# Running the first layernorm statistics one tile ahead of the second in a transformer block's preparation stage

## The chip, the cores and the metric

The kernel runs on all 8 NeuronCores of one Trainium2 chip. Each core computes one element of the batch on its own, with no exchange between cores. The metric is the device time in microseconds (us) of the slowest core. A core has these engines, each with its own in-order instruction queue: TensorE (PE in the profile, its weight loads PEld), VectorE (DVE), ScalarE (ACT), GpSimd (POOL) and SyncE (SP, which here issues DMA transfers). ScalarE issues DMAs too (ACTq). Engines wait for each other by semaphores.

## The reference, cut to what matters

x is 8 x 4096 x 2048 in float32; a core has one 4096 x 2048 part of it.

```python
xn = _layernorm(x, axis=-1)                    # (x - mean) / sqrt(var + 1e-5)
x = x + attn(xn, Wq, bq, Bq, Aq, ..., Ao) + ffn(xn, gamma, beta, weight, bias, alpha)

# attn: q, k, v, out projections with rank-16 LoRA updates, 16 heads of 128, softmax
# ffn:
mu = jnp.mean(x, axis=-1, keepdims=True)       # x is xn here: a second layernorm
var = jnp.mean(jnp.square(x - mu), axis=-1, keepdims=True)
xn = (x - mu) * jax.lax.rsqrt(var + LN_EPS) * gamma + beta
a = jnp.sign(xn)
signed_w = jnp.sign(weight - jnp.mean(weight, axis=1, keepdims=True))
out = (jnp.einsum('bsi,oi->bso', a, signed_w) + bias) * alpha
```

So each row of x is normalized once for the attention (LN1), and the result is normalized again (LN2), scaled, shifted and reduced to its sign for the ffn.

## The kernel before, in words

The program is a list of stages (`_phase0` to `_phase5`), each written out as straight code for all engines. Between two stages `_join` lets every engine wait for all semaphores, so no stage overlaps the next. `_phase0` loads constants and transposes the small LoRA matrices. `_phase1`, which the change touches, makes both normalized inputs. `_phase2` computes the q, k and v projections, `_phase3` the attention, `_phase4` the output projection and `_phase5` the ffn product.

`_phase1` first broadcasts gamma and beta to all partitions (`gb_g`, `gb_b`). Then it walks over NT = 32 tiles of 128 rows x 2048 columns. For tile t:

- SP loads the float32 rows of the next tile into `xf[(t+1)%2]` (L296), once the last readers of that buffer are through.
- `stats_pass` on `xf` (LN1): VectorE sums the row (L242), makes the mean (L244) and its negative (L246). ScalarE squares the centred row with an accumulated sum (L252, `Square`; the squared row itself goes into a scratch tile that nobody reads, here `abf`). VectorE divides by D (L258); ScalarE takes Ln (L260) and Exp with -0.5 (L263), which give 1/sqrt(var + eps). VectorE makes the offset (L266).
- VectorE writes the normalized row `xn32` (L304).
- `stats_pass` on `xn32` (LN2): the same lines again, with `xnbf` as scratch. Between its Square and its Ln, ScalarE copies `xn32` to bfloat16 `xnbf` (L312, handed in as `mid=_cast`).
- VectorE normalizes `xn32` in place (L319), multiplies by gamma (L323) and adds beta (L325). ScalarE writes its sign to `abf` (L327).
- TensorE transposes `xnbf` in 16 blocks through the PSUM tiles `ptrA` and `ptrB` (L333, L345), ScalarE copies them out into `xn_fm` (L338, L350). The same happens with `abf` (L359, L373) into `a_acc` (L366, L378). Every second tile, ScalarE issues the store of `a_acc` to `s_a` (L389).

All the small per-row statistics lie in the eight columns of one tile, `stat`. The order of work on each engine is the order in which the code stands: nothing reorders it.

Of the kernel before, what the change touches and what calls it, by code (L numbers as in the profile page):

```python
# [34 lines left out]
def build_nc(T, D):  # L35
# [3 lines left out]
    NT = T // 128  # L39
# [3 lines left out]
    INV_D = 1.0 / D  # L43
# [5 lines left out]
    nc = bass.Bass("TRN2", target_bir_lowering=False)  # L49
# [176 lines left out]
    def _phase1(sync):  # L226
        ldx = [S("p1_ldx0"), S("p1_ldx1")]
        dv = S("p1_dv")
        ac = S("p1_ac")
        pe = S("p1_pe")  # L230
        sta = S("p1_sta")
        evA = S("p1_evA")
        evB = S("p1_evB")
        xf_last = {}
        abf_free = [0]
        xnbf_free = [0]

        def stats_pass(src, scratch, act_dv_wait=None, act_pe_wait=None,
                       dv_wait=None, mid=None):
            if dv_wait is not None:  # L240
                nc.vector.wait_ge(dv.h, dv_wait)
            v_sum = dv.inc(nc.vector.reduce_sum(stat[:, 0:1], src, axis=AX.X))  # L242
            nc.vector.wait_ge(dv.h, v_sum)
            v_mu = dv.inc(nc.vector.tensor_scalar_mul(stat[:, 2:3], stat[:, 0:1], INV_D))  # L244
            nc.vector.wait_ge(dv.h, v_mu)
            v_nm = dv.inc(nc.vector.tensor_scalar_mul(stat[:, 3:4], stat[:, 2:3], -1.0))  # L246
# [5 lines left out]
            a_sq = ac.inc(nc.scalar.activation(scratch, src, AF.Square,  # L252
                                               bias=stat[:, 3:4],
                                               accum_out=stat[:, 1:2]))
            if mid is not None:
                mid()
            nc.vector.wait_ge(ac.h, a_sq)
            v_var = dv.inc(nc.vector.tensor_scalar_mul(stat[:, 4:5], stat[:, 1:2], INV_D))  # L258
            nc.scalar.wait_ge(dv.h, v_var)
            a_ln = ac.inc(nc.scalar.activation(stat[:, 7:8], stat[:, 4:5], AF.Ln,  # L260
                                               bias=EPS))
            nc.scalar.wait_ge(ac.h, a_ln)
            a_r = ac.inc(nc.scalar.activation(stat[:, 5:6], stat[:, 7:8], AF.Exp,  # L263
                                              scale=-0.5))
# [21 lines left out]
        sync.wait_ge(pe.h, pe.v)  # L286
        ldx[0].dinc(sync.dma_start(xf[0].ap(), x_d.ap()[0:128, :]))

        for t in range(NT):
# [9 lines left out]
            nc.vector.wait_ge(ldx[sl].h, ldx[sl].v)  # L299
            nc.scalar.wait_ge(ldx[sl].h, ldx[sl].v)  # L300
# [6 lines left out]
            xf_last[t] = (v_xn, a_sq1)  # L307
# [6 lines left out]
            v_nmr2, a_sq2 = stats_pass(xn32.ap(), xnbf.ap(), act_dv_wait=v_xn,  # L314
                                       act_pe_wait=xnbf_free[0], dv_wait=v_xn,
                                       mid=_cast)
            nc.vector.wait_ge(dv.h, v_xn)
# [881 lines left out]
```

## Time and profile before

| what | value |
|---|---|
| median of 3 runs | 8460.73 us (8460.21 to 8728.11) |
| time of the profiled execution | 8459.73 us |
| its span, first to last instruction of the slowest core | 8457.9 us |
| spans of the 8 cores | 8446.6 to 8457.9 us |
| mean granted TensorE clock, every core | 0.838 |
| busy share of the span: PE, PEld, DVE, ACT | 66%, 26%, 37%, 32% |
| stages by start, from the timeline | `_phase1` loop 136 us, `_phase2` 953 us, `_phase3` about 2850 us, `_phase4` and `_phase5` from about 7000 us |

The profile is of one execution, on its slowest core; its span is 1.8 us shorter than the time measured for that execution. "Busy" is the time in which an engine executes; what it waited for stands in brackets behind an instruction of the timeline. The granted clock is 1.00 for TensorE's full 2.4 GHz and 0.50 for 1.2 GHz, averaged over a stretch.

### The profile page before, as it was taken

The numbers are of one execution on the slowest core, as the hardware profiler recorded it, in microseconds if no ns is written. First come the engines' busy times: TensorE is split into PE (matmuls) and PEld (weight loads), VectorE is DVE, ScalarE is ACT, GpSimd is POOL, SyncE is SP. The second block draws the span as 40 slices with busy tenths as digits, with TensorE's granted clock in tenths as the row PEclk, the third lists the DMA queues.
The fourth block names the chain that finished last, engine by engine and source line by source line (L and its number), as shares of the span: only waits on it lengthen the run. The fifth ranks groups of instructions, "written<-read, shape, count | busy, mean of one in ns | idle before, by whom it ended". The sixth has DMA issues, their size and how long they took to land.

```text
span 8457.9 us, 66068 instructions; the slowest of 8 cores (8446.6 to 8457.9 us)
## 1 busy us (share of the span) xinstructions
PE 5556.4 (66%) x22685; PEld 2235.6 (26%) x23096; DVE 3161.8 (37%) x2750; ACT 2664.3 (32%) x2610; POOL 3.7 (0%) x17
## 2 busy tenths in 40 slices
PE   1111488888888766666666666666666665996499
PEld 0111233333333222222222222222222222332243
DVE  3555311211111244444444444444444444113433
ACT  1444200000000255455555555555555552000000
POOL 0000000000000000000000000000000000000000
PEclk9999989889898877777777777777777776997699
DMA  1111111111111100000000000000000003442344
GB/s 35 60 64 60 52 58 52 57 53 52 56 54 56 46 19 5 19 20 19 19 15 9 19 19 20 19 5 19 19 20 19 5 4 115 149 149 103 126 167 149
DMA packets 171860, 424.87 MB, mean 50 GB/s; under 512 B 26005, under 2 KB 107925, under 8 KB 142869
## 3 DMA queue, kind: packets, MB, share of 16 engines
q1 hardware_dynamic: 80922, 269.60, 9.7%
q10 hardware_dynamic: 90624, 151.02, 4.8%
q8 instruction: 204, 3.34, 0.2%
q14 instruction: 110, 0.90, 0.0%
HBM read 269.58 MB, written 150.99 MB: 50 GB/s over the span
## 4 chain that ended last, share of the span: by engine, by line
PE 55%; DVE 23%; issue 11%; ACT 8%; DMA 1%; ACTq 1%; DVEq 1%; SPq 0%
PE sg L743 11%; PE avp L778 9%; PE pgB L502 8%; PE pgA L502 8%; DVE ptree L810 7%; PE pa L945 5%; PE pf L1111 5%; ACT pT L766 4%; DVE ptree L802 3%; DVE rec L622 3%; PE ptrW L480 1%; DVE obuf L613 1%; PE avp L616 1%; DVE stat L242 1%; DVE xn L323 1%
## 5 line engine op out<-in xcount | busy, mean ns | idle before, releaser
L766 ACT ACTIVATE pT<-sg,negc 128x1024 bf16<-128x1024 f32 x2048 | 2100.3, 1132 | 1699.3 <-DVE ostg L601 1504.7
L743 PE MATMUL sg<-qT,kT 128*128 128x512 bf16 x3997 | 1335.3, 427 | 492.4 <-ACT pT L766 480.6
L778 PE MATMUL avp<-pT,vh 128*128 128x512 bf16 x4019 | 1313.5, 413 | 112.1 <-ACT pT L766 105.6
L789 DVE TENSOR_TENSOR ptree<-pT 128x4096 bf16<-128x4096 bf16 x128 | 293.4, 2292 | 1762.3 <-ACT pT L766 1762.3
L743 PEld LDWEIGHTS sg<-qT,kT 128*128 128x128 bf16 x4096 | 389.4, 105 | 1318.3 <-issue 1076.8
L502 PE MATMUL pgB<-xn_fm,wT 128*128 128x512 bf16 x3000 | 706.7, 398 | 42.1 <-DVE wT L487 34.5
L502 PE MATMUL pgA<-xn_fm,wT 128*128 128x512 bf16 x3000 | 706.4, 398 | 41.8 <-DVE wT L487 34.1
L664 ACT ACTIVATE sq<-kT 128x4096 bf16<-128x4096 bf16 x16 | 58.9, 3683 | 1876.8 <-DMA qT<-s_qT 1876.8
L810 DVE TENSOR_TENSOR ptree<-ptree 128x4096 bf16<-128x4096 bf16 (+3 forms) x512 | 593.1, 1158 | 64.4 <-DVE ptree L802 23.1
L778 PEld LDWEIGHTS avp<-pT,vh 128*128 128x128 bf16 x4096 | 409.0, 106 | 777.1 <-issue 469.2
L616 PE MATMUL avp<-ptree,ones_bfc 128*1 128x512 bf16 x128 | 74.9, 585 | 723.4 <-DVE obuf L613 723.4
L622 DVE RECIPROCAL rec<-avp 1x512 f32<-1x512 f32 x128 | 428.2, 3346 | 107.6 <-PE avp L616 107.6
L945 PE MATMUL pa<-woT,o_sp 128*128 128x512 bf16 x2000 | 458.9, 380 | 11.3 <-ACT oBs L927 8.3
L1111 PE MATMUL pf<-swT,a_sp 128*128 128x512 bf16 x2005 | 456.3, 381 | 8.1 <-issue 6.6
L502 PEld LDWEIGHTS pgB<-xn_fm,wT 128*128 128x128 bf16 x3072 | 306.8, 102 | 436.4 <-issue 120.7
L502 PEld LDWEIGHTS pgA<-xn_fm,wT 128*128 128x128 bf16 x3072 | 306.8, 102 | 435.9 <-issue 119.8
L802 DVE TENSOR_TENSOR ptree<-pT 128x4096 bf16<-128x4096 bf16 x128 | 293.4, 2292 | 220.9 <-ACT pT L766 220.9
L333 PE MATMUL ptrA<-ident,xnbf 128*128 128x128 bf16 x256 | 32.4, 307 | 443.5 <-ACT stat L260 415.9
L594 PE MATMUL avp<-rec,ones_f32r 1*128 1x512 f32 x256 | 265.1, 1136 | 1.6 <-DVE rec L622 1.6
L945 PEld LDWEIGHTS pa<-woT,o_sp 128*128 128x128 bf16 x2048 | 189.9, 98 | 273.1 <-issue 61.5
L963 DVE TENSOR_TENSOR res<-pa,x_sp 128x1024 f32<-128x1024 f32 x64 | 78.4, 1224 | 486.7 <-PE pa L955 472.1
L1111 PEld LDWEIGHTS pf<-swT,a_sp 128*128 128x128 bf16 x2048 | 190.2, 98 | 243.2 <-issue 32.8
(120 smaller groups left out, 3276.5 us busy)
## 6 DMA issues: line engine op xcount, KB each, us to landing
xf<-x SPq DMA_DIRECT2D x32, 1024.0 KB, 4.9
x_sp<-x SPq DMA_DIRECT2D x32, 1024.0 KB, 6.5
out<-res ACTq DMA_DIRECT2D x64, 512.0 KB, 4.6
ord<-out SPq DMA_DIRECT2D x32, 1024.0 KB, 6.6
out<-res4b ACTq DMA_DIRECT2D x64, 512.0 KB, 4.4
s_a<-a_acc ACTq DMA_DIRECT2D x16, 1024.0 KB, 5.7
wbuf<-wq SPq DMA_DIRECT2D x16, 1024.0 KB, 5.9
wbuf<-wk SPq DMA_DIRECT2D x16, 1024.0 KB, 6.0
```

What stands on the lines that cost most here:

```text
L502: pe.inc(nc.tensor.matmul(pg[:, k * 512:(k + 1) * 512], wT[sl][:, ic * 128:(ic + 1) * 128], xn_fm[:, ic * T + tc * 512: ic * T + (tc + 1) ...
L594: pv = pe.inc(nc.tensor.matmul(avp[cur_qsl][:], ones_f32r.ap(), rec2[pqsl][0:1, :], start=True, stop=True))
L616: ptree_mm[pqsl] = pe.inc(nc.tensor.matmul(avp[pqsl][0:1, 0:512], ones_bfc.ap(), ptree2[pqsl][:, 0:512], start=True, stop=True, skip_group ...
L622: v_rec = dv.inc(nc.vector.reciprocal(rec2[pqsl][0:1, :], avp[pqsl][0:1, 0:512]))
L743: ins = nc.tensor.matmul(sg3[b][:, j * 512:(j + 1) * 512], kT_b[sl][:, kt * 128:(kt + 1) * 128], qT_b[sl][:, qq0:qq0 + 512], start=True, s ...
L766: e = ac.inc(nc.scalar.activation(pT2[qsl][:, g * 1024:(g + 1) * 1024], sg3[s_bank[g]][:], AF.Exp, bias=negc2[sl].ap()))
L778: pe.inc(nc.tensor.matmul(avp[qsl][:], vh2[sl][:, kt * 128:(kt + 1) * 128], pT2[qsl][:, kt * 512:(kt + 1) * 512], start=(kt == 0), stop=(k ...
L789: tree_a[0] = dv.inc(nc.vector.tensor_tensor(ptree2[qsl][:, 0:wq // 2], pT2[qsl][:, 0:wq // 2], pT2[qsl][:, wq:wq + wq // 2], ALU.add))
L802: v_part = dv.inc(nc.vector.tensor_tensor(ptree2[qsl][:, w // 2:w], pT2[qsl][:, w // 2:w], pT2[qsl][:, w + w // 2:2 * w], ALU.add))
L810: v_part = dv.inc(nc.vector.tensor_tensor(ptree2[qsl][:, 0:w // 2], ptree2[qsl][:, 0:w // 2], ptree2[qsl][:, w // 2:w], ALU.add))
L945: pe.inc(nc.tensor.matmul(pa[psl][:, ocs * 512:(ocs + 1) * 512], o_sp[sl][:, ic * 512 + tt * 128: ic * 512 + tt * 128 + 128], woT[:, ic * ...
L1111: pe.inc(nc.tensor.matmul(pf[psl][:, ocs * 512:(ocs + 1) * 512], a_sp[sl][:, ic * 512 + tt * 128: ic * 512 + tt * 128 + 128], swT[:, ic * ...
```

## The change

`stats_pass` is cut in two: `stats_head` (sum, mean, negative mean, Square and, where given, the copy) and `stats_tail` (variance, Ln, Exp, offset). LN2 gets a statistics tile of its own, `stat2`. The head of LN1 for tile t+1 is put behind the head of LN2 for tile t. The tail of LN1 for tile t+1 stands behind the Sign of tile t. The normalization of tile t+1 (`vxn[t+1]`) is the last thing in the body of tile t, behind the transposes and the evictions. LN1's Square now writes its unused squares in float32 into the other `xf` buffer (`xf[1 - s]`) instead of in bfloat16 into `abf`. The load of x for tile t+1 waits for LN1's Square of tile t, since that writes into the buffer that is loaded. Line numbers below are of the changed file.

```diff
+    stat2 = es_p1.enter_context(nc.sbuf_tensor("stat2", [128, 8], F32))
...
+        def stats_head(src_ap, scratch, sb, act_dv_wait=None, act_pe_wait=None,
+                       dv_wait=None, mid=None, nm_ac_wait=None):
...
+            if nm_ac_wait:
+                nc.vector.wait_ge(ac.h, nm_ac_wait)
+            v_nm = dv.inc(nc.vector.tensor_scalar_mul(sb[:, 3:4], sb[:, 2:3], -1.0))
...
+        def ln1_head(t, pe_wait=None):
+            s = t % 2
+            nc.vector.wait_ge(ldx[s].h, ldx[s].v)
+            nc.scalar.wait_ge(ldx[s].h, ldx[s].v)
+            return stats_head(
+                xf[s].ap(), xf[1 - s].ap(), stat,
+                act_dv_wait=(vxn[t - 1] if t >= 1 else None),
+                act_pe_wait=pe_wait,
+                nm_ac_wait=(sq1[t - 1] if t >= 1 else 0))
...
             if t + 1 < NT:
                 if t >= 1:
-                    pdv, pac = xf_last[t - 1]
-                    sync.wait_ge(dv.h, pdv)
-                    sync.wait_ge(ac.h, pac)
+                    sync.wait_ge(dv.h, vxn[t - 1])
+                sync.wait_ge(ac.h, sq1[t])
                 ldx[(t + 1) % 2].dinc(sync.dma_start(
...
-            v_nmr, a_sq1 = stats_pass(xf[sl].ap(), abf.ap(),
-                                      act_pe_wait=abf_free[0])
-            nc.vector.wait_ge(dv.h, v_nmr)
-            v_xn = dv.inc(nc.vector.tensor_scalar(
-                xn32.ap(), xf[sl].ap(), stat[:, 5:6], stat[:, 6:7],
-                ALU.mult, ALU.add))
...
+            a_sq2 = stats_head(xn32.ap(), xnbf.ap(), stat2,
+                               act_dv_wait=vxn[t], act_pe_wait=xnbf_free[0],
+                               dv_wait=vxn[t], mid=_cast,
+                               nm_ac_wait=sq2_prev[0])
+            sq2_prev[0] = a_sq2
+            if t + 1 < NT:
+                sq1[t + 1] = ln1_head(t + 1)
+            v_nmr2 = stats_tail(stat2, a_sq2)
...
             nc.scalar.wait_ge(dv.h, v_b)
+            nc.scalar.wait_ge(pe.h, abf_free[0])
             a_s = ac.inc(nc.scalar.activation(abf.ap(), xn32.ap(), AF.Sign))
+            if t + 1 < NT:
+                nmr1[t + 1] = stats_tail(stat, sq1[t + 1])
...
+            if t + 1 < NT:
+                nc.vector.wait_ge(dv.h, nmr1[t + 1])
+                nc.vector.wait_ge(ac.h, a_s)
+                vxn[t + 1] = dv.inc(nc.vector.tensor_scalar(
+                    xn32.ap(), xf[(t + 1) % 2].ap(), stat[:, 5:6], stat[:, 6:7],
+                    ALU.mult, ALU.add))
```

VectorE's queue before, from the LN1 normalization of tile 1 to the sum of the next tile's x; `xf0` and `xf1` are the two load buffers, `p1_dv`, `p1_ac`, `p1_pe` count what VectorE, ScalarE and TensorE have done:

```order
L304 TENSOR_SCALAR xn32<-xf1,stat 128x2048 [waits p1_dv]
L242 TENSOR_REDUCE stat<-xn32 128x1 [waits p1_dv]
L244 TENSOR_SCALAR stat<-stat 128x1 [waits p1_dv]
L246 TENSOR_SCALAR stat<-stat 128x1 [waits p1_dv]
L258 TENSOR_SCALAR stat<-stat 128x1 [waits p1_ac]
L266 TENSOR_SCALAR stat<-stat 128x1 [waits p1_ac]
L319 TENSOR_SCALAR xn32<-xn32,stat 128x2048 [waits p1_dv]
L323 TENSOR_TENSOR xn32<-xn32,gb_g 128x2048 [waits p1_dv]
L325 TENSOR_TENSOR xn32<-xn32,gb_b 128x2048 [waits p1_dv]
L242 TENSOR_REDUCE stat<-xf0 128x1 [waits p1_ldx0]
```

The same stretch of VectorE's queue in the changed kernel:

```order
L422 TENSOR_SCALAR xn32<-xf1,stat 128x2048 [waits p1_dv,p1_ac]
L246 TENSOR_REDUCE stat2<-xn32 128x1 [waits p1_dv]
L248 TENSOR_SCALAR stat2<-stat2 128x1 [waits p1_dv]
L252 TENSOR_SCALAR stat2<-stat2 128x1 [waits p1_dv,p1_ac]
L246 TENSOR_REDUCE stat<-xf0 128x1 [waits p1_ldx0]
L248 TENSOR_SCALAR stat<-stat 128x1 [waits p1_dv]
L252 TENSOR_SCALAR stat<-stat 128x1 [waits p1_dv,p1_ac]
L267 TENSOR_SCALAR stat2<-stat2 128x1 [waits p1_ac]
L275 TENSOR_SCALAR stat2<-stat2 128x1 [waits p1_ac]
L341 TENSOR_SCALAR xn32<-xn32,stat2 128x2048 [waits p1_dv]
L345 TENSOR_TENSOR xn32<-xn32,gb_g 128x2048 [waits p1_dv]
L347 TENSOR_TENSOR xn32<-xn32,gb_b 128x2048 [waits p1_dv]
```

The sum over the next tile's x moved from behind the beta addition to the place between LN2's negative mean and LN2's variance; the variance and offset of that next tile follow behind the beta addition.

ScalarE's queue before, from the bfloat16 copy of tile 1 to the Ln of tile 2:

```order
L312 ACTIVATE xnbf<-xn32 128x2048 [waits p1_ac]
L260 ACTIVATE stat<-stat 128x1 [waits p1_dv]
L263 ACTIVATE stat<-stat 128x1 [waits p1_ac]
L327 ACTIVATE abf<-xn32 128x2048 [waits p1_dv]
L338 ACTIVATE xn_fm<-ptrA 128x8x128 [waits p1_pe]
L350 ACTIVATE xn_fm<-ptrB 128x8x128 [waits p1_pe]
L366 ACTIVATE a_acc<-ptrA 128x8x128 [waits p1_pe]
L378 ACTIVATE a_acc<-ptrB 128x8x128 [waits p1_pe]
L389 DMA s_a<-a_acc 128x16x256 [waits p1_evA,p1_evB]
L252 ACTIVATE abf,stat<-xf0,stat 128x2048 [waits p1_ldx0,p1_pe,p1_dv]
L260 ACTIVATE stat<-stat 128x1 [waits p1_dv]
```

The same stretch of ScalarE's queue in the changed kernel:

```order
L328 ACTIVATE xnbf<-xn32 128x2048 [waits p1_ac]
L258 ACTIVATE xf1,stat<-xf0,stat 128x2048 [waits p1_ldx0,p1_dv]
L269 ACTIVATE stat2<-stat2 128x1 [waits p1_dv]
L272 ACTIVATE stat2<-stat2 128x1 [waits p1_ac]
L350 ACTIVATE abf<-xn32 128x2048 [waits p1_dv,p1_pe]
L269 ACTIVATE stat<-stat 128x1 [waits p1_dv]
L272 ACTIVATE stat<-stat 128x1 [waits p1_ac]
L363 ACTIVATE xn_fm<-ptrA 128x8x128 [waits p1_pe]
L375 ACTIVATE xn_fm<-ptrB 128x8x128 [waits p1_pe]
L391 ACTIVATE a_acc<-ptrA 128x8x128 [waits p1_pe]
L403 ACTIVATE a_acc<-ptrB 128x8x128 [waits p1_pe]
L414 DMA s_a<-a_acc 128x16x256 [waits p1_evA,p1_evB]
```

The next tile's Square moved from behind the evictions and the store to the place between the copy and LN2's Ln; the next tile's Ln and Exp stand between the Sign and the evictions. TensorE's queue is the same in both kernels, and SP's has the same transfers with the one changed wait.

## Rows read from the trace of the kernel before

**Rows 1.** Windows of core 0: busy us (and count) PE, PEld, DVE, ACT, POOL; PEclk, DMA, GB/s

```profile
136.00:952.00 816.00, 121.33 (x1024) 101.77 (x1024) 419.43 (x448) 397.21 (x448) 0.00 (x0) 1.00 0.19 60
952.00:1400.00 448.00, 383.14 (x1716) 171.21 (x1749) 78.77 (x64) 4.74 (x8) 0.00 (x0) 0.91 0.17 55
...
2400.00:2850.00 450.00, 388.72 (x1741) 171.45 (x1775) 85.41 (x68) 0.00 (x0) 0.00 (x0) 0.90 0.15 49
...
2950.00:3600.00 650.00, 411.90 (x1417) 144.34 (x1444) 299.43 (x224) 345.29 (x332) 0.00 (x0) 0.76 0.04 14
```

**Rows 2.** The tile `xf`: durations in ns min/median/max, first and last start in us

```profile
L304 DVE TENSOR_SCALAR xn<-xf,stat x32: 1345/1346/1347, 142.2 to 925.8; 128x2048 f32<-128x2048 f32 x32
...
DMA to landing us min/median/max: 4.7/4.9/9.2
```

**Rows 3.** Timeline of one tile that issues no store: start us, us, instruction

```profile
304.87 2.29 DVE L323 TENSOR_TENSOR xn<-xn,gb_g 128x2048 f32<-128x2048 f32 x1
307.27 2.29 DVE L325 TENSOR_TENSOR xn<-xn,gb_b 128x2048 f32<-128x2048 f32 x1
309.48 2.28 DVE L242 TENSOR_REDUCE stat<-xf 128x1 f32<-128x2048 f32 x1
309.65 1.91 ACT L327 ACTIVATE abf<-xn 128x2048 bf16<-128x2048 f32 x1 [6.66 <-DVE xn L325]
311.47 1.01 ACT L338 ACTIVATE xn_fm<-ptrA 128x1024 bf16<-128x1024 bf16 x1
...
313.78 1.02 ACT L366 ACTIVATE a_acc<-ptrA 128x1024 bf16<-128x1024 bf16 x1 [0.40 <-PE ptrA L359]
...
315.61 2.00 ACT L252 ACTIVATE abf<-xf,stat 128x2048 bf16<-128x2048 f32 x1
317.50 0.20 ACT L252 ACTIVATION_READ_ACCUMULATOR abf<-xf,stat 128x1 f32 x1
...
318.05 0.20 ACT L260 ACTIVATE stat<-stat 128x1 f32<-128x1 f32 x1 [0.35 <-DVE stat L258]
318.35 0.20 ACT L263 ACTIVATE stat<-stat 128x1 f32<-128x1 f32 x1
318.65 0.21 DVE L266 TENSOR_SCALAR stat<-stat 128x1 f32<-128x1 f32 x1 [0.70 <-ACT stat L263]
318.98 1.34 DVE L304 TENSOR_SCALAR xn<-xf,stat 128x2048 f32<-128x2048 f32 x1
320.42 2.29 DVE L242 TENSOR_REDUCE stat<-xn 128x1 f32<-128x2048 f32 x1
...
322.81 0.15 DVE L244 TENSOR_SCALAR stat<-stat 128x1 f32<-128x1 f32 x1
323.07 0.15 DVE L246 TENSOR_SCALAR stat<-stat 128x1 f32<-128x1 f32 x1
323.32 2.00 ACT L252 ACTIVATE xnbf<-xn,stat 128x2048 bf16<-128x2048 f32 x1 [4.78 <-DVE stat L246]
...
325.51 1.91 ACT L312 ACTIVATE xnbf<-xn 128x2048 bf16<-128x2048 f32 x1
...
327.32 0.19 ACT L260 ACTIVATE stat<-stat 128x1 f32<-128x1 f32 x1
```

**Rows 4.** Timeline of a tile that issues the store, ScalarE only

```profile
338.54 1.02 ACT L366 ACTIVATE a_acc<-ptrA 128x1024 bf16<-128x1024 bf16 x1 [0.34 <-PE ptrA L359]
...
340.56 0.37 ACTq L389 DMA_DIRECT2D s_a<-a_acc  x1
341.13 2.00 ACT L252 ACTIVATE abf<-xf,stat 128x2048 bf16<-128x2048 f32 x1 [0.66 <-ACT a_acc L378]
```

**Rows 5.** Timeline of `_phase2`: a VectorE conversion that writes bfloat16

```profile
960.50 1.23 DVE L471 CAST wbf<-wbuf 128x2048 bf16<-128x2048 f32 x1 [19.33 <-DMA wbuf<-wq]
```

**Rows 6.** Cores: us from first to last instruction, mean granted TensorE clock

```profile
core 0: 8457.9 us, clock 0.838
...
core 4: 8446.6 us, clock 0.838
```

More of the change, by code:

```diff
@@ L233, in _phase1 @@
         evB = S("p1_evB")
-        xf_last = {}
         abf_free = [0]
         xnbf_free = [0]
-        def stats_pass(src, scratch, act_dv_wait=None, act_pe_wait=None,
-                       dv_wait=None, mid=None):
+        vxn = {}
+        sq1 = {}
+        nmr1 = {}
+        sq2_prev = [0]
+        def stats_head(src_ap, scratch, sb, act_dv_wait=None, act_pe_wait=None,
+                       dv_wait=None, mid=None, nm_ac_wait=None):
             if dv_wait is not None:
                 nc.vector.wait_ge(dv.h, dv_wait)
-            v_sum = dv.inc(nc.vector.reduce_sum(stat[:, 0:1], src, axis=AX.X))
+            v_sum = dv.inc(nc.vector.reduce_sum(sb[:, 0:1], src_ap, axis=AX.X))
             nc.vector.wait_ge(dv.h, v_sum)
-            v_mu = dv.inc(nc.vector.tensor_scalar_mul(stat[:, 2:3], stat[:, 0:1], INV_D))
+            v_mu = dv.inc(nc.vector.tensor_scalar_mul(sb[:, 2:3], sb[:, 0:1], INV_D))
             nc.vector.wait_ge(dv.h, v_mu)
-            v_nm = dv.inc(nc.vector.tensor_scalar_mul(stat[:, 3:4], stat[:, 2:3], -1.0))
+            if nm_ac_wait:
+                nc.vector.wait_ge(ac.h, nm_ac_wait)
+            v_nm = dv.inc(nc.vector.tensor_scalar_mul(sb[:, 3:4], sb[:, 2:3], -1.0))
             if act_pe_wait is not None:
@@ L251, in stats_pass, with stats_tail @@
             nc.scalar.wait_ge(dv.h, v_nm)
-            a_sq = ac.inc(nc.scalar.activation(scratch, src, AF.Square,
-                                               bias=stat[:, 3:4],
-                                               accum_out=stat[:, 1:2]))
+            a_sq = ac.inc(nc.scalar.activation(scratch, src_ap, AF.Square,
+                                               bias=sb[:, 3:4],
+                                               accum_out=sb[:, 1:2]))
             if mid is not None:
                 mid()
+            return a_sq
+        def stats_tail(sb, a_sq):
             nc.vector.wait_ge(ac.h, a_sq)
-            v_var = dv.inc(nc.vector.tensor_scalar_mul(stat[:, 4:5], stat[:, 1:2], INV_D))
+            v_var = dv.inc(nc.vector.tensor_scalar_mul(sb[:, 4:5], sb[:, 1:2], INV_D))
             nc.scalar.wait_ge(dv.h, v_var)
-            a_ln = ac.inc(nc.scalar.activation(stat[:, 7:8], stat[:, 4:5], AF.Ln,
+            a_ln = ac.inc(nc.scalar.activation(sb[:, 7:8], sb[:, 4:5], AF.Ln,
                                                bias=EPS))
             nc.scalar.wait_ge(ac.h, a_ln)
-            a_r = ac.inc(nc.scalar.activation(stat[:, 5:6], stat[:, 7:8], AF.Exp,
+            a_r = ac.inc(nc.scalar.activation(sb[:, 5:6], sb[:, 7:8], AF.Exp,
                                               scale=-0.5))
@@ L266, in stats_pass @@
             v_nmr = dv.inc(nc.vector.tensor_scalar(
-                stat[:, 6:7], stat[:, 2:3], stat[:, 5:6], -1.0, ALU.mult, ALU.mult))
-            return v_nmr, a_sq
+                sb[:, 6:7], sb[:, 2:3], sb[:, 5:6], -1.0, ALU.mult, ALU.mult))
+            return v_nmr
+        def ln1_head(t, pe_wait=None):
[7 more added lines that the diff above has]
+                nm_ac_wait=(sq1[t - 1] if t >= 1 else 0))
         gld = S("p1_gld")
@@ L287, in _phase1 @@
         ldx[0].dinc(sync.dma_start(xf[0].ap(), x_d.ap()[0:128, :]))
+        sq1[0] = ln1_head(0, pe_wait=pe.v)
+        nmr1[0] = stats_tail(stat, sq1[0])
+        nc.vector.wait_ge(dv.h, nmr1[0])
+        vxn[0] = dv.inc(nc.vector.tensor_scalar(
+            xn32.ap(), xf[0].ap(), stat[:, 5:6], stat[:, 6:7],
+            ALU.mult, ALU.add))
         for t in range(NT):
@@ L292, in _phase1 @@
                 if t >= 1:
-                    pdv, pac = xf_last[t - 1]
-                    sync.wait_ge(dv.h, pdv)
-                    sync.wait_ge(ac.h, pac)
+                    sync.wait_ge(dv.h, vxn[t - 1])
+                sync.wait_ge(ac.h, sq1[t])
                 ldx[(t + 1) % 2].dinc(sync.dma_start(
                     xf[(t + 1) % 2].ap(), x_d.ap()[(t + 1) * 128:(t + 2) * 128, :]))
-            nc.vector.wait_ge(ldx[sl].h, ldx[sl].v)
-            nc.scalar.wait_ge(ldx[sl].h, ldx[sl].v)
-            v_nmr, a_sq1 = stats_pass(xf[sl].ap(), abf.ap(),
-                                      act_pe_wait=abf_free[0])
-            nc.vector.wait_ge(dv.h, v_nmr)
-            v_xn = dv.inc(nc.vector.tensor_scalar(
-                xn32.ap(), xf[sl].ap(), stat[:, 5:6], stat[:, 6:7],
-                ALU.mult, ALU.add))
-            xf_last[t] = (v_xn, a_sq1)
             xnbf_cp = [0]
@@ L313, in _cast @@
                                                          AF.Copy))
[L314 to L317, printed above, removed]
+            a_sq2 = stats_head(xn32.ap(), xnbf.ap(), stat2,
[6 more added lines that the diff above has]
+            v_nmr2 = stats_tail(stat2, a_sq2)
+            nc.vector.wait_ge(dv.h, vxn[t])
             nc.vector.wait_ge(dv.h, v_nmr2)
             v_u = dv.inc(nc.vector.tensor_scalar(
-                xn32.ap(), xn32.ap(), stat[:, 5:6], stat[:, 6:7],
+                xn32.ap(), xn32.ap(), stat2[:, 5:6], stat2[:, 6:7],
                 ALU.mult, ALU.add))
@@ L392, in _phase1 @@
                     aac_v))
+            if t + 1 < NT:
[3 more added lines that the diff above has]
+                    xn32.ap(), xf[(t + 1) % 2].ap(), stat[:, 5:6], stat[:, 6:7],
+                    ALU.mult, ALU.add))
         sync.wait_ge(ldx[0].h, ldx[0].v)
```

## The prediction
> **What bounds the kernel now.** I read the windows by stage first. The stage of the change runs from 136 to 952 us, 816 us or 9.6% of the span, and in it no engine is half busy except VectorE at 419 of 816 us (51%); ScalarE has 397 us (49%), TensorE 121 us [rows 1]. No engine is the bound there, so the bound is a chain of waits that goes back and forth between engines. No other stage is edited, and the stages are kept apart by a wait of all engines for all semaphores; so the change can only shorten this stage, unless it changes what the clock does later.
>
> The length of one turn of that chain comes from the instruction that occurs once per tile, the LN1 normalization: 32 of them, the first at 142.2, the last at 925.8 us, so 783.6 / 31 = 25.28 us per tile [rows 2]. What stands in those 25 us is read from the timeline of one tile [rows 3], as start-to-start steps, since these hold the waits too. From beta to beta, the chain is: beta addition, Sign, four evictions (with a wait for the second transposes in their middle), Square of LN1, Ln, Exp, offset, normalize, sum, mean, negative mean, Square of LN2, copy, Ln, Exp, offset, normalize, gamma, beta. One part of LN1 is already hidden: the sum of the next x starts at 309.48, beside the Sign that starts at 309.65, and is over before ScalarE reaches the Square. Moving it earns nothing.
>
> **The change as a new chain.** I follow the orders of the two queues from one LN1 normalization (time 0) to the next. Each step is a difference of starts in [rows 3].
>
> - Normalize to sum: 318.98 to 320.42, 1.44. Sum to mean 2.39, mean to negative mean 0.26, to LN2's Square 0.25. The Square can start at 4.34.
> - Square to copy 2.19 (323.32 to 325.51), copy to the next ScalarE instruction 1.81 (325.51 to 327.32). At 8.34 this next instruction is now LN1's Square of the next tile, not Ln. Its input is there: VectorE takes the sum of x right behind LN2's negative mean, from about 4.2, and has mean and negative mean by about 7.1.
> - That Square holds ScalarE from its start to its accumulator read, 1.89 (315.61 to 317.50), and the read 0.20 more. LN2's Ln stands behind it and starts at 10.43. The copy's old neighbour is late by 2.09 us: this is what the change pays.
> - Ln to Exp 0.30, Exp to offset 0.30, offset to normalize 0.33 (all from the rows at 318.05 to 318.98), normalize to gamma 1.44 (as normalize to sum), gamma to beta 2.40, beta to Sign 2.38. The Sign starts at 17.58.
> - Sign to the next ScalarE instruction 1.82, then again Ln to Exp, Exp to offset and offset to normalize, 0.93 together. LN1's variance needs only a sum long finished and VectorE is free behind the beta addition, so Ln need not wait for it. The next normalization starts at 20.33.
>
> Compared with the turn before: the four evictions leave the chain (311.47 to 315.61, 4.14), LN1's Square and the hop to VectorE and back leave it (315.61 to 318.05, 2.44), and 2.09 comes back between copy and Ln. Net 4.49 us per tile.
>
> **Do the evictions stay hidden?** They now run on ScalarE beside normalize, sum and mean. They begin behind Exp, about 0.53 before time 0 (0.63 from Exp to normalize, less 0.10 until ScalarE is free). They take 4.14 to the end of that stretch, so ScalarE is free at 3.61; LN2's Square wants it at 4.34. Cover left: 0.73 us. In every second tile the store is issued behind them: from the third eviction to the Square it is 2.59 us with the store [rows 4] against 1.83 without (313.78 to 315.61), 0.76 more. Then ScalarE is free at 4.37, 0.03 late. So the store, which before cost 0.76 in half of the tiles (0.37 on average, 15 stores between 31 steps), costs almost nothing: 0.35 more is saved. If the cover were gone altogether, each us of lateness would cost 31 us in the whole.
>
> The step of 25.28 holds 24.82 for a tile as in rows 3 (20.05 from beta at 307.27 to Ln at 327.32, and 0.30, 0.30, 0.33, 1.44 and 2.40 back to beta), 0.37 of store and 0.09 of stray delays, which I keep. New step: 20.33 + 0.02 + 0.09 = 20.44. Saved: 25.28 - 20.44 = 4.84 per tile, times 31 steps = 150 us. The head of tile 0 still runs alone before the first step and the end of tile 31 is as before, so the other parts of the stage stay.
>
> **What else is issued.** The load of x for tile t+1 is issued after LN1's Square of tile t, at about 10.4 in tile t-1's turn; its first reader comes at 4.2 of tile t's turn, 14.2 us later. It lands in 4.9, at most 9.2 us [rows 2]; SP has nothing else queued in this stage. Behind the load's new wait nothing else stands. VectorE's new wait ahead of the negative mean is for a Square of the previous tile, long done; the normalization's new wait for the Sign is over before Exp is, which stands behind the Sign on ScalarE. ScalarE's new wait ahead of the Sign, for the previous tile's transposes, is some 15 us old. I put all of these at 0; a satisfied wait more may cost up to the 0.04 to 0.05 that a hop shows beyond its duration, 0 to 2 us in the whole for the single one on the chain.
>
> **LN1's Square in float32.** No row shows ScalarE writing 2048 float32 values to SBUF. Below, it is bounded by the 1.91 of the same width without an accumulator (-0.09); above, by twice the 2.00 if the written bytes set the time (+2.00). The nearest row is VectorE's: bfloat16 output takes 1.23 where float32 output takes 1.34 [rows 3, 5], so it is some 10% at most there. ScalarE reads float32 here and keeps 2.00 with any of its sources. I take 0. The range in the sum: -3 to +62 us (31 times). The Trainium skill (page "ScalarE: Activation LUTs", section "What ACT_TABLE_LOAD costs") says that an activation takes one element per cycle and lane in float32 and bfloat16 alike, and gives about 280 ns + 0.833 ns per element, 1.99 us at 2048; this trace agrees for bfloat16 output with 2.00. By that page the term is 0, by the byte bound it is 62 us.
>
> **New overlaps.** Normalize and sum run beside evictions now. The nearest overlap before is the sum of x beside the Sign: 2.28, against 2.29 for the sum of `xn32` alone [rows 3]. So 0, and not below. The Trainium skill ("SBUF — State Buffer", section "SBUF: two separate sides") says that only a port pair shared by VectorE and GpSimd makes engines wait; that page would also give 0, and GpSimd is idle in this stage (0.00, rows 1).
>
> **Sum.** 8459.73 of the profiled execution minus 150 is 8310; it was 1.0 below the median of the runs, so I forecast **8311 us**, 1.8% less. About 2% (169 us) is what a measurement of this kernel can tell from no change; this gain lies just inside it. To pass it, the step would have to come to 25.28 - 169 / 31 = 19.82 us.
>
> **The rivals.**
>
> - *ScalarE's queue comes late.* The evictions, the store or the second transposes push LN2's Square past 4.34. For: only 0.73 us of cover, none with the store. Against: their 4.14 is measured with the same waits in it. Late by 1 us in each tile gives 8311 + 31 = 8342.
> - *Float32 squares are slow*, at the byte bound: 8311 + 62 = 8373. Still faster than before.
> - *The delay of 2.09 does not show.* If Square, accumulator read and Ln overlapped so that LN2's tail came at its old time, the step would be 18.35 and the time 8311 - 65 = 8246, 2.5% faster. Against: ScalarE takes its queue in order, and the Ln behind the copy starts at 327.32, 0.10 ahead of the copy's end and no sooner [rows 3].
> - *It doesn't do what it says.* If the sum of x had to wait for the load, nothing would be gained (8460). For that, the landing would have to take over 14.2 us; 9.2 is the longest.
> - *The other side: the clock of `_phase2`.* The granted clock is 1.00 in this stage, 0.91 falling to 0.90 in the projections, 0.76 in attention, where TensorE is busy 412 of 650 us [rows 1]. If a shorter and denser stage ahead left the projections with attention's 0.76, their 1898 us (952 to 2850) would grow by 1898 x (0.90 / 0.76 - 1) = 350 us, and the time would be 8661, 2.4% slower. It decides from where the growth eats the 150 us: below a clock of 0.90 / (1 + 150 / 1898) = 0.83. Against: the clock is nearly the same in the first and the last piece of the projections, 1450 us apart, so it doesn't remember what came before; and the eight cores, with whatever timing each has, lie within 11 us and at one clock [rows 6].
>
> **How the numbers follow.** Forecast 0.84, late queue 0.06, slow squares 0.04, hidden delay 0.02, no effect 0.02, clock 0.02. The forecast's own spread is from small terms: the store's tiles (0 to 0.4 per pair more, up to 6 us), the 10% of the VectorE row applied to Square (6 us), stray delays 0 to 0.2 per tile (3 us either way), and up to 11 us that cores differ by in the unedited stages. The range of 8292 to 8345 holds these and the late queue; the byte bound and the two far cases are left out. Faster by over 2%: 0.04 (the hidden delay, and a little for small terms that all go one way); slower by over 2%: 0.02 (the clock); within 2%: 0.94.
>
> **What would show it.** In the changed profile, the LN1 normalizations (L422 for 31 of them) should start 20.4 to 20.5 us apart, and `_phase2` should begin at about 803 us in place of 953. In a tile's timeline, LN1's Square should stand between the copy and LN2's Ln and take 2.0 us, with Ln about 2.1 us after it starts; ScalarE should wait for VectorE's negative mean by about 0.7 us ahead of LN2's Square in tiles without store, and not at all in those with one; VectorE should wait some 3.8 us for LN2's Exp. The clock of the projections should stay at 0.89 to 0.91. I am wrong if Square shows more than 2.1 us, if the evictions end after 4.4 us of the turn, if sums or normalizations run longer beside them than 2.29 and 1.35, or if a stage behind changes its length.

## The result

| | before | changed |
|---|---|---|
| median of the 10 executions of each in this comparison, us | 8656.75 | 8570.32 |
| lowest | 8460.21 | 8313.34 |
| profiled execution | 8459.73 | 8313.34 |
| its span | 8457.9 | 8311.6 |
| ratio (of 3 executions changed to 4 before, see below), 95% interval | | 0.9822 [0.9783, 0.9861] |

Six of the ten executions before and seven of the ten changed ones took 125 to 400 us more than the lowest, in the changed kernel always with the cores of one die or both at a lower granted TensorE clock; the ratio is of the others, 8460 to 8501 us before and 8313 to 8333 after.

Against the lowest changed execution the forecast of 8311 us was 2 us off, and the ratio says 1.8% faster, as forecast. Its interval excludes "no change", but does not tell whether the gain is above or below 2%. The forecast's range (8292 to 8345) does not hold the median of 8570.32; what that says of the forecast comes below.

**Profile after.** The windows of the slowest core, cut at the same places of the program as [rows 1]; columns as there:

```profile
136.00:803.00 667.00, 121.26 (x1024) 101.58 (x1024) 415.91 (x448) 392.34 (x448) 0.00 (x0) 1.00 0.23 74
803.00:1251.00 448.00, 390.75 (x1747) 171.25 (x1748) 78.79 (x64) 4.74 (x8) 0.00 (x0) 0.91 0.17 55
...
2251.00:2701.00 450.00, 395.98 (x1768) 171.00 (x1767) 85.44 (x68) 0.00 (x0) 0.00 (x0) 0.90 0.14 48
2801.00:3451.00 650.00, 413.97 (x1445) 143.28 (x1446) 299.50 (x224) 345.45 (x333) 0.00 (x0) 0.76 0.04 14
```

The stage takes 667 us in place of 816, with the same work in it: VectorE 416 us busy against 419, ScalarE 392 against 397. Nearly all of the time that went was waiting. The stages behind kept their clock, 0.91, 0.90 and 0.76, to the digit.

The tile `xf` (durations ns min/median/max, first and last start us), answering to [rows 2]:

```profile
L258 ACT ACTIVATE xf<-xf,stat x32: 1985/1986/2001, 138.2 to 764.0; 128x2048 f32<-128x2048 f32 x32
...
L422 DVE TENSOR_SCALAR xn<-xf,stat x31: 1345/1347/1348, 161.9 to 776.2; 128x2048 f32<-128x2048 f32 x31
...
L311 DVE TENSOR_SCALAR xn<-xf,stat x1: 1346/1346/1346, 141.6 to 141.6; 128x2048 f32<-128x2048 f32 x1
...
DMA to landing us min/median/max: 4.8/5.0/6.5
```

The normalization of tile 0 is now a line of its own (L311, 141.6), the others are L422 up to 776.2: (776.2 - 141.6) / 31 = 20.47 us per tile, against 25.28 before and 20.44 forecast. LN1's Square takes 1.986 us with float32 output, no more than the 2.00 with bfloat16.

The timeline of one tile without store, answering to [rows 3]:

```profile
324.49 0.19 ACT L269 ACTIVATE stat<-stat 128x1 f32<-128x1 f32 x1
324.77 0.20 ACT L272 ACTIVATE stat<-stat 128x1 f32<-128x1 f32 x1
324.88 1.01 ACT L363 ACTIVATE xn_fm<-ptrA 128x1024 bf16<-128x1024 bf16 x1
325.08 0.21 DVE L275 TENSOR_SCALAR stat<-stat 128x1 f32<-128x1 f32 x1 [2.48 <-ACT stat L272]
325.47 1.35 DVE L422 TENSOR_SCALAR xn<-xf,stat 128x2048 f32<-128x2048 f32 x1 [0.18 <-DVE stat L275]
...
326.92 2.29 DVE L246 TENSOR_REDUCE stat<-xn 128x1 f32<-128x2048 f32 x1
...
328.11 1.02 ACT L403 ACTIVATE a_acc<-ptrB 128x1024 bf16<-128x1024 bf16 x1
329.31 0.15 DVE L248 TENSOR_SCALAR stat<-stat 128x1 f32<-128x1 f32 x1
329.64 0.15 DVE L252 TENSOR_SCALAR stat<-stat 128x1 f32<-128x1 f32 x1 [0.17 <-DVE stat L248]
329.74 2.29 DVE L246 TENSOR_REDUCE stat<-xf 128x1 f32<-128x2048 f32 x1
329.88 2.00 ACT L258 ACTIVATE xnbf<-xn,stat 128x2048 bf16<-128x2048 f32 x1 [0.76 <-DVE stat L252]
...
332.07 1.91 ACT L328 ACTIVATE xnbf<-xn 128x2048 bf16<-128x2048 f32 x1
...
333.89 1.99 ACT L258 ACTIVATE xf<-xf,stat 128x2048 f32<-128x2048 f32 x1
...
335.78 0.18 ACT L258 ACTIVATION_READ_ACCUMULATOR xf<-xf,stat 128x1 f32 x1
335.87 0.18 ACT L269 ACTIVATE stat<-stat 128x1 f32<-128x1 f32 x1
336.15 0.20 ACT L272 ACTIVATE stat<-stat 128x1 f32<-128x1 f32 x1
336.46 0.21 DVE L275 TENSOR_SCALAR stat<-stat 128x1 f32<-128x1 f32 x1 [3.73 <-ACT stat L272]
```

Read it from 325.47. The evictions (L363 to L403) run beside the normalization and the sum; they are over at 329.13, and ScalarE then waits 0.76 us for VectorE's negative mean: that is the cover. The prediction's 0.73 counts from where the next instruction could have started, 0.91 us behind the start of the last eviction; by that count the cover is 0.86 us (329.02 to 329.88). Then comes the price: between the copy (332.07) and Ln (335.87) stands LN1's Square (333.89), and VectorE waits 3.73 us for the Exp behind it. Square to Ln is 1.98 us.

### The profile page after: what moved, and what is told of

It reads as the page before. It is cut to its first block, busy times and chain, and to the rows that moved or that the text cites. A ratio compares the mean times of both kernels' runs of the same rounds, so it can differ in the third digit from the quotient of the medians.

```text
span 8311.6 us, 66605 instructions; the slowest of 8 cores (8300.6 to 8311.6 us)
## 1 busy us (share of the span) xinstructions
PE 5622.4 (68%) x23096; PEld 2233.0 (27%) x23096; DVE 3159.9 (38%) x2750; ACT 2658.9 (32%) x2610; POOL 3.7 (0%) x17
## 4 chain that ended last, share of the span: by engine, by line
PE 56%; DVE 25%; issue 10%; ACT 6%; DMA 1%; ACTq 1%; DVEq 1%; SPq 0%
PE sg L775 11%; PE avp L810 9%; PE pgB L534 9%; PE pgA L534 9%; DVE ptree L842 7%; PE pf L1143 6%; PE pa L977 5%; ACT pT L798 4%; DVE ptree L834 4%; DVE rec L654 3%; DVE stat L246 2%; PE ptrW L512 1%; DVE obuf L645 1%; PE avp L648 1%; DVE xn L345 1%
## 5 line engine op out<-in xcount | busy, mean ns | idle before, releaser
L775 PE MATMUL sg<-qT,kT 128*128 128x512 bf16 x4096 | 1355.6, 427 | 478.8 <-ACT pT L798 478.2
L534 PE MATMUL pgB<-xn_fm,wT 128*128 128x512 bf16 x3072 | 727.4, 399 | 27.4 <-DVE wT L519 27.4
L534 PE MATMUL pgA<-xn_fm,wT 128*128 128x512 bf16 x3072 | 726.1, 399 | 25.3 <-DVE wT L519 25.3
L384 PE MATMUL ptrA<-ident,abf 128*128 128x128 bf16 x256 | 32.4, 306 | 329.6 <-ACT xn_fm L363 329.6
```

The source lines that it names most:

```text
L534: pe.inc(nc.tensor.matmul(pg[:, k * 512:(k + 1) * 512], wT[sl][:, ic * 128:(ic + 1) * 128], xn_fm[:, ic * T + tc * 512: ic * T + (tc + 1) ...
L775: ins = nc.tensor.matmul(sg3[b][:, j * 512:(j + 1) * 512], kT_b[sl][:, kt * 128:(kt + 1) * 128], qT_b[sl][:, qq0:qq0 + 512], start=True, s ...
```

## The experiments

Seven variants were run, two of them again, and the changed kernel twice more. In each, the step is (last start - first start) / 31 of the LN1 normalizations in its profile. All that differs is in `_phase1` (and, for two normalized tiles, in the buffers of `_phase0`), so by the prediction a step that differs by s moves the time by 31 s. The first four below ran on one chip, three of them only once; beside them the kernel before took 8458.99 to 8463.52 us in seven executions. On the two chips of the later runs its lowest times were 8459.51 and 8460.29 us, so times of different chips can be compared within a few us.

**Evictions back on the chain, LN1's head still ahead.**

```diff
             a_s = ac.inc(nc.scalar.activation(abf.ap(), xn32.ap(), AF.Sign))
-            if t + 1 < NT:
-                nmr1[t + 1] = stats_tail(stat, sq1[t + 1])
...
             if t + 1 < NT:
+                nmr1[t + 1] = stats_tail(stat, sq1[t + 1])
                 nc.vector.wait_ge(dv.h, nmr1[t + 1])
```

> The changed kernel with LN1's tail (variance, Ln, Exp, offset) behind the evictions and the store instead of ahead of them: undoes the part of the change that took the evictions off the chain, and keeps LN1's head ahead. Theory: 4.14 us of evictions and 0.38 us of store on average come back, step about 25.0 us, time about 8453 us, nearly that of the kernel before. Rival (the head computed ahead is the gain): step at most 22.9 us, time at most 8389 us.

Measured: 8452.48 us, step (915.1 - 143.0) / 31 = 24.91. ScalarE's part of its timeline:

```profile
309.99 1.91 ACT L350 ACTIVATE abf<-xn 128x2048 bf16<-128x2048 f32 x1 [6.92 <-DVE stat L267]
311.80 1.00 ACT L361 ACTIVATE xn_fm<-ptrA 128x1024 bf16<-128x1024 bf16 x1
...
315.94 0.20 ACT L269 ACTIVATE stat<-stat 128x1 f32<-128x1 f32 x1
```

Ln comes 5.95 us behind the Sign's start in place of 1.81, the 4.14 of the evictions more. With LN1's Square computed ahead and the evictions on the chain, only 7 of the gain's 146 us are left (8459.73 to 8452.48). So the evictions' leaving is the gain; computing the statistics ahead is not, by itself.

**LN1's Square back behind the Sign, evictions still hidden.** The head is cut once more: its VectorE part stays, its ScalarE part is a function `sq1_issue` that is called later. It shows whether the Square had to move at all.

```diff
             if t + 1 < NT:
-                sq1[t + 1] = ln1_head(t + 1)
+                sq1_issue = ln1_head(t + 1, defer=True)
             v_nmr2 = stats_tail(stat2, a_sq2)
...
             if t + 1 < NT:
+                sq1[t + 1] = sq1_issue()
                 nmr1[t + 1] = stats_tail(stat, sq1[t + 1])
```

> The changed kernel, but with LN1's Square of the next tile issued behind the Sign instead of between the copy and LN2's Ln. Theory (the gain is the four evictions that left the chain; where the Square stands is nearly a wash): between copy and Ln 1.98 us go, between Sign and Ln 2.44 us come (Square, accumulator read, the hop to VectorE and back), so the step from one LN1 normalization to the next grows from 20.47 to 20.93 us and the time from 8313 to about 8327 us. Rival (the gain is that the Square is computed ahead): putting it back behind the Sign gives back 2.4 us per tile or more, step at least 22.9, time at least 8389 us.

Measured: 8329.33 us, step (791.6 - 142.7) / 31 = 20.93. So the new place of the Square is worth only 0.46 us of the 4.81 gained: it takes the Square and the hop to VectorE and back from behind the Sign (2.44), and puts 1.98 between copy and Ln.

**LN1's Square behind LN2's Exp**, into ScalarE's longest idle time.

```diff
             if t + 1 < NT:
-                sq1[t + 1] = ln1_head(t + 1)
+                sq1_issue = ln1_head(t + 1, defer=True)
             v_nmr2 = stats_tail(stat2, a_sq2)
+            if t + 1 < NT:
+                sq1[t + 1] = sq1_issue()
```

> The changed kernel, but with LN1's Square issued behind LN2's Exp, where ScalarE stands idle for 6.7 us before the Sign. Theory (the Square's place between copy and Ln costs its whole length on the chain): the step falls by 1.98 to 18.49 us and the time by 61 to about 8252 us. Rival (the delay was covered by VectorE's own work, the sum of the next x): step and time stay, 20.47 and 8313 us.

Measured: 8252.52 us (median of four), ratio to the kernel before 0.9754 [0.9738, 0.9770], step (716.0 - 142.6) / 31 = 18.50. The timeline of one turn, ScalarE's and VectorE's lines around the moved Square:

```profile
315.23 1.91 ACT L334 ACTIVATE xnbf<-xn 128x2048 bf16<-128x2048 f32 x1
...
317.05 0.19 ACT L275 ACTIVATE stat<-stat 128x1 f32<-128x1 f32 x1
317.32 0.20 ACT L278 ACTIVATE stat<-stat 128x1 f32<-128x1 f32 x1
...
317.52 2.00 ACT L263 ACTIVATE xf<-xf,stat 128x2048 f32<-128x2048 f32 x1
317.63 0.21 DVE L281 TENSOR_SCALAR stat<-stat 128x1 f32<-128x1 f32 x1 [1.75 <-ACT stat L278]
```

Ln starts 1.82 behind the copy again, and VectorE waits 1.75 us for the Exp instead of 3.73. Nothing had covered the 1.98 us that the change had put on the chain, and this reordering gives them back: 61 us.

**One more eviction.** The last eviction of a tile is done twice, the second behind a wait for the first.

```diff
                     ptrB[:].rearrange("p (c n) -> p c n", n=128)[:, 0:NCH - 8, :],
                     AF.Copy))
+                nc.scalar.wait_ge(evB.h, evB.v)
+                evB.inc(nc.scalar.activation(
+                    aac_v[:, 8:NCH, (t % 2) * 128:(t % 2) * 128 + 128],
...
```

> The changed kernel with the last eviction of a tile done twice (the same values to the same place), behind a wait for the first. It takes about 0.92 and a hop of 0.2 us. Theory (the evictions are hidden with a cover of 0.76 us in tiles without store and 0.16 us in those with one): LN2's Square is late by about 0.35 and 0.95 us, 0.65 on average, step 21.1 us, time about 8333 us. Rival without cover: the full 1.1 us per tile, step 21.6, 8347 us. Rival with ample cover: nothing, 20.47 and 8313 us.

Measured: 8330.18 us, step (793.7 - 141.2) / 31 = 21.05, 0.58 more; 0.65 was expected. ScalarE's lines in a tile with store and in one without:

```profile
312.55 1.02 ACT L408 ACTIVATE a_acc<-ptrB 128x1024 bf16<-128x1024 bf16 x1
313.65 0.37 ACTq L419 DMA_DIRECT2D s_a<-a_acc  x1
314.23 2.00 ACT L258 ACTIVATE xnbf<-xn,stat 128x2048 bf16<-128x2048 f32 x1 [0.66 <-ACT a_acc L408]
...
333.96 1.02 ACT L408 ACTIVATE a_acc<-ptrB 128x1024 bf16<-128x1024 bf16 x1
334.88 1.99 ACT L258 ACTIVATE xnbf<-xn,stat 128x2048 bf16<-128x2048 f32 x1
```

Neither Square waits for VectorE any more: the releaser is the eviction ahead of it or nobody. The extra eviction costs 1.11 us of ScalarE and 0.58 us of the chain, so half of it fell into the cover; the rival without cover wanted the whole. With covers of 0.86 without the store and 0.15 with it (below), the lateness should be 0.25 and 0.96 us, about 0.6 on average.

**Without the three added waits.**

```diff
-            if nm_ac_wait:
-                nc.vector.wait_ge(ac.h, nm_ac_wait)
             v_nm = dv.inc(nc.vector.tensor_scalar_mul(sb[:, 3:4], sb[:, 2:3], -1.0))
...
                 nc.vector.wait_ge(dv.h, nmr1[t + 1])
-                nc.vector.wait_ge(ac.h, a_s)
```

> The changed kernel without the three waits that were added on VectorE for ScalarE's counts (ahead of the two negative means and of the normalization), each of which is implied by an earlier wait for a later count. Theory (a second semaphore on one instruction costs a hop of 0.07 us, though its count was reached long ago): the negative mean of LN2 and the normalization start 0.07 us sooner each, step 20.33, time about 8309 us. Rival (a satisfied wait is free): step 20.47, time 8313 us.

Measured: step (769.6 - 140.1) / 31 = 20.31 against 20.47; the profiled execution took 8303.97 us, the other two 8570.69 and 8576.00. VectorE in its timeline:

```profile
322.17 0.21 DVE L273 TENSOR_SCALAR stat<-stat 128x1 f32<-128x1 f32 x1 [2.49 <-ACT stat L270]
322.49 1.35 DVE L419 TENSOR_SCALAR xn<-xf,stat 128x2048 f32<-128x2048 f32 x1
...
326.33 0.15 DVE L248 TENSOR_SCALAR stat<-stat 128x1 f32<-128x1 f32 x1
326.59 0.15 DVE L250 TENSOR_SCALAR stat<-stat 128x1 f32<-128x1 f32 x1
```

Offset to normalization is 0.32 us here and 0.39 in the changed kernel (325.08 to 325.47); mean to negative mean is 0.26 here and 0.33 there (329.31 to 329.64). A satisfied second wait cost 0.07 us each time, and two of these three were on the chain. A fourth added wait, ScalarE's for the transposes ahead of the Sign, stayed in this run. The Sign starts 2.44 us behind the beta addition in it and in the changed kernel, and 2.38 before. That wait is the only one added at this link, but no run took it out, so that it costs the 0.06 is not shown.

**LN1's tail ahead of the Sign.** As the kernel with the Square behind Exp, and:

```diff
+        def tail_act(sb, a_sq):
+            nc.scalar.wait_ge(ac.h, a_sq)
+            a_ln = ac.inc(nc.scalar.activation(sb[:, 7:8], sb[:, 1:2], AF.Ln,
+                                               bias=EPS, scale=INV_D))
...
                 sq1[t + 1] = sq1_issue()
+                a_r1 = tail_act(stat, sq1[t + 1])
...
             v_b = dv.inc(nc.vector.tensor_tensor(xn32.ap(), xn32.ap(), gb_b.ap(), ALU.add))
+            if t + 1 < NT:
+                nmr1[t + 1] = tail_dv(stat, a_r1)
```

> As the run with the Square behind LN2's Exp, and further: Ln takes the sum of squares with scale 1/D, so that the variance step on VectorE goes; LN1's Ln and Exp follow its Square at once; LN1's offset stands behind the beta addition; the redundant waits on VectorE's negative means are gone. Theory: what is left behind the Sign is only the hop to the next normalization, which must wait because it overwrites what the Sign reads. Sum of the links: 17.5 us; the evictions start 0.17 before the turn and leave 0.39 of cover, so the store's tiles are 0.37 late, 0.18 on average; step about 17.8, time about 8230 us. Rival (the evictions' cover is gone and they set the pace): each tile late by 1 us, step 18.7 or more, no better than the 8252 us of that run.

> The kernel of e6_tail_ahead_of_sign again. Its profile showed a step of 17.74 us. Theory (each us of the step is 31 us of the time, and no other stage changes): 8313 - 31 x (20.47 - 17.74) = 8228 us, ratio 0.9726. Rival (a denser first stage costs the later stages clock): over 8240 us with a granted clock below 0.83.

Measured: steps of (690.2 - 140.2) / 31 = 17.74 and (692.3 - 142.4) / 31 = 17.74, against 17.8 forecast. The medians were 8499.94 and 8501.28 us, with one die or both at a granted clock of 0.76 to 0.81 in all ten executions. So by its letter the rival of the second run (over 8240 us, a clock below 0.83) is what the whole times show, and the ratio on record, 1.005, sets such executions beside others at 0.838. In the four of the second run's executions in which one die was granted 0.833, that die's slowest core had a span of 8228.5 to 8232.0 us, which is what the step says: these cores ran the same denser stage. Whether a denser first stage makes the lower clock more frequent is left open; the counts come at the end.

**Two normalized tiles.** As the last, with a second tile `xn32b` for the scaled and shifted values, LN2's tail ahead of the copy, and the Sign behind the evictions into `xn_fm`.

```diff
+    xn32b = es_p1.enter_context(nc.sbuf_tensor("xn32b", [128, D], F32))
...
-                xn32.ap(), xn32.ap(), stat2[:, 5:6], stat2[:, 6:7],
+                xn32b.ap(), xn32.ap(), stat2[:, 5:6], stat2[:, 6:7],
...
-                nc.vector.wait_ge(ac.h, a_s)
+                nc.vector.wait_ge(ac.h, xnbf_cp[0])
```

> As e6, with a second tile for the scaled and shifted values, so that the next normalization need not wait for the Sign and LN2's Ln need not wait for the copy; the Sign stands behind the evictions of xn_fm (the small buffers of the first stage share memory to make room). Theory: VectorE's chain is normalize, sum, mean, negative mean, LN2's Square, Ln, Exp, offset, normalize, gamma, beta, offset: 13.9 us. ScalarE ends the last eviction about 4.8 us into the next turn against 4.36 when its Square is wanted, with the store 5.6: late by 0.8 on average. Step about 14.8, time about 8137 us. Rival (ScalarE sets the pace with gaps of its own): step 16 or more, time at least 8175 us.

> The kernel of e7_two_normalized_tiles again. Its profile showed a step of 14.98 us. Theory: 8313 - 31 x (20.47 - 14.98) = 8143 us, ratio 0.9625. Rival (a denser first stage costs the later stages clock): over 8155 us with a granted clock below 0.83.

Measured: first 8414.09 us in the profiled execution, with four cores at a clock of 0.76 and the other four at 0.831 with spans up to 8137.6 us, and a step of 14.98. In the second run all eight cores were granted 0.831 or 0.832 in the profiled execution: 8138.65 us and a step of (606.9 - 143.6) / 31 = 14.95. That is 3.8% less than the 8460.29 us of the fastest execution of the kernel before on that chip. It rests on this one execution; the other four took 8284.23 to 8508.39 us, with a lower clock on one die or both. The waits of the loop (who waited for whom: us in total, times, longest), first two of the changed kernel:

```profile
ACT abf L350 <- DVE stat L267: 210.1, 31, 7.0
DVE stat L275 <- ACT stat L272: 193.7, 62, 4.0
```

and those of this one:

```profile
ACT a_acc L416 <- PE ptrA L409: 41.5, 30, 1.4
DVE stat L295 <- ACT stat L290: 33.1, 30, 1.5
ACT abf L404 <- DVE stat L295: 17.2, 29, 0.9
ACT xnbf L273 <- ACT a_acc L428: 9.9, 15, 0.7
```

VectorE's waiting for the Exp is down to 33 us from the 194 us of the changed kernel, ScalarE's before the Sign to 17 us from 210. ScalarE's largest wait is now the one for the transposes of `abf`, which start only behind the Sign: 41.5 us, against 10.9 in the changed kernel. What is left is a loop in which both are at work most of the time. By the windows of that execution VectorE is 408 of 499 us busy and ScalarE 394:

```profile
136.00:635.00 499.00, 121.99 (x1031) 105.38 (x1032) 408.14 (x384) 394.02 (x448) 0.00 (x0) 1.00 0.31 100
635.00:1083.00 448.00, 384.35 (x1727) 171.49 (x1758) 78.78 (x64) 4.74 (x8) 0.00 (x0) 0.91 0.17 55
```

The projections behind it run at 0.91 as in [rows 1]. So in this execution a stage 39% shorter ahead of them cost them no clock.

**The changed kernel again, twice.**

> The changed kernel itself, beside the one before on one chip. Theory (the step of 25.28 us fell to 20.47): 8313 us, ratio 0.9825. Rival (part of the gain hung on the chip or the pairing of the first measurement): a ratio outside 0.980 to 0.985.

> The changed kernel beside the one before, for a comparison on another chip. Theory: 20.47 us per step, 8313 us, ratio 0.9825. Rival: a ratio outside 0.980 to 0.985.

Measured first: a ratio of 0.9796 [0.9711, 0.9881], too wide to tell 0.980 from 0.985; its lowest three executions took 8311.59, 8312.37 and 8316.28 us, the lowest two of the kernel before there 8459.51 and 8461.05, and the step was (776.4 - 141.7) / 31 = 20.47 again. The second time, on another chip, all five executions took 8573.04 to 8660.02 us, with a lower clock on one die or both, and no ratio came out; the step was (778.2 - 143.7) / 31 = 20.47 even so.

All steps and times together:

| kernel | step, us | time, us | which execution | 8313.3 + 31 x (step - 20.47) |
|---|---|---|---|---|
| before | 25.28 | 8459.73 | the profiled one | 8462 |
| tail behind evictions | 24.91 | 8452.48 | the only one | 8451 |
| one more eviction | 21.05 | 8330.18 | the only one | 8331 |
| Square behind Sign | 20.93 | 8329.33 | the only one | 8328 |
| changed | 20.47 | 8313.34 | the profiled one | |
| no extra waits | 20.31 | 8303.97 | lowest of 3 | 8308 |
| Square behind Exp | 18.50 | 8252.52 | median of 4 | 8252 |
| two normalized tiles | 14.95 | 8138.65 | lowest of 5 | 8142 |

One line with the slope 31 runs through all of them within 5 us. In every execution of the table all eight cores had a granted clock of 0.83 to 0.84.

## Why the prediction was right, and where it was wrong

- **The stage is bound by a chain between engines, not by one of them.** Right: the stage lost 149 us, while VectorE's busy time fell by 4 us and ScalarE's by 5.
- **New chain of 20.33, step of 20.44.** Measured 20.47, and 20.40 from one normalization to the next in a tile without a stray delay (305.07 to 325.47). That it came this near is partly luck, since the links that were off nearly cancelled. Ln starts 0.09 us behind the accumulator read and not 0.20. Against that, the prediction put added waits at 0 and allowed for a single one on the chain; two on VectorE lay on it and cost 0.07 us each (without VectorE's three the step fell by 0.16), and the link from beta to Sign, where a third was added, grew by 0.06.
- **Evictions leave (4.14), the Square's length comes back (2.09).** Right and shown: the first by the run with the tail behind the evictions, the second (1.98 measured) by the run with the Square behind Exp. The third term, 2.44 for LN1's Square and its hop, is borne out by the run with the Square behind the Sign (20.93 - 20.47 = 2.44 - 1.98).
- **The cover of 0.73, none with the store.** Measured 0.86 without the store, by the prediction's count. With it 0.15 was left and not 0.03 too little: ScalarE was free at 4.27 and not 4.37 of the turn, and the Square was wanted at 4.42 and not 4.34, of which 0.07 is the second wait ahead of the negative mean. The extra eviction showed both covers at work.
- **Float32 squares.** The value taken (0) was right, the byte bound (+62 us) fell: 1.986 us. The rule of the Trainium skill named in the prediction (ScalarE: Activation LUTs, section "What ACT_TABLE_LOAD costs"), one element per cycle in either format, agrees.
- **Overlaps cost nothing.** Right: beside the evictions the sum takes 2.29 and the normalization 1.35 us, as before.
- **The step that failed** is the last term of the sum, from the profile to the median: "it was 1.0 below the median of the runs, so I forecast 8311 us". This term of 1.0 us measured 257 us (8570.32 - 8313.34); for the kernel before it was 197 us (8656.75 - 8459.73). The range was made only of the kernel's own small terms and of the 11 us by which cores differ in one execution, though the table of times had one execution of three at 8728.11 us.
- **What stood in that term, and the clock rival.** A trace of the changed kernel from the second repetition shows it. The slowest core of the profiled execution here (8311.6 us), then that of the repetition (8576.5 us); windows as in [rows 1], and the first Square of the attention's keys:

```profile
L696 ACT ACTIVATE sq<-kT x16: 3616/3685/3692, 2721.6 to 6649.2; 128x4096 bf16<-128x4096 bf16 x16
...
803.00:1251.00 448.00, 393.50 (x1522) 160.80 (x1523) 69.53 (x57) 4.75 (x8) 0.00 (x0) 0.78 0.15 51
2801.00:3451.00 650.00, 468.75 (x1633) 176.78 (x1631) 241.72 (x189) 249.93 (x234) 0.00 (x0) 0.70 0.07 26
...
L696 ACT ACTIVATE sq<-kT x16: 3607/3613/3698, 2986.1 to 6917.5; 128x4096 bf16<-128x4096 bf16 x16
```

  The loop has the same step in both, 20.47. The projections are granted 0.78 in place of 0.91, with TensorE busy 394 of 448 us as against 391, and from LN1's first Square to the attention it takes 2845.8 us in place of 2583.4. These 262 us are nearly all of the 265 by which the spans differ. That is the mechanism of the prediction's clock rival, which put 350 us on a clock of 0.76 and gave it 0.02. But the change is not needed for it: the kernel before has the same excess, for example 8726.76 us with one die at 0.79 and 8461.05 with none, on one chip. The argument against it, that all cores lie at one clock, came from one execution.
- **What stays open.** What makes the chip grant a lower clock is not shown, nor that the change leaves its frequency alone. On the two chips of the later runs, some cores were below the clock of the other executions in 15 of 20 executions of the kernel before, 9 of 12 of the changed one, and 20 of 21 of the two kernels with the tail ahead of the Sign and with two normalized tiles. These are too few to tell whether a denser first stage matters.

## What to carry to other kernels

In a stage bound by a chain across engines, write the new chain link by link from start-to-start differences, in each engine's queue order: what gains is the work that leaves the chain (here the evictions), and what is moved "ahead" can land between two links of it and cost its whole length. Look for the queue's longest idle time and put the moved piece there; here that was two positions further down, and worth 61 us more. Once the loop's step is known, the number of steps times its difference gave the time of every variant here within 5 us, in executions in which all eight cores were granted 0.83 to 0.84. So a profile can compare variants even where whole-kernel times scatter; but a forecast of a median needs the scatter of the times in its range, too.

## What the runs showed of the hardware

- An instruction whose second semaphore had been reached long before started 0.07 us later than with one wait: 0.33 against 0.26 us and 0.39 against 0.32 us on VectorE.
- Behind an accumulator read, an instruction that doesn't depend on it started 0.09 us after the read's start (335.78 to 335.87 us), so the read held the queue for half of its own 0.18 us.
- Issuing the store held ScalarE's queue 0.58 us from the issue to the next Square's start (313.65 to 314.23 us).
- With the same kernel, two cores of one die were granted 0.78 and two 0.91 in the projections of one execution (cores 4 and 5, cores 6 and 7 of the second repetition, 803 to 1251 us).
